# Relative attention layers: five PSUM slots for transposed scores and jobs, one pair of banks for the row-maximum scores

## The chip, the cores and the metric

The kernel runs on one core of a Trainium2 chip. The metric is the device time of one execution in microseconds (us); "the span" is the time from the first to the last instruction of the one execution that was profiled. PE is TensorE, DVE is VectorE, ACT is ScalarE, POOL is GpSimd, SP is the engine that issues most DMAs.

## The reference, cut to what matters

Four attention layers stand one behind the other on 8 images of 32 x 32 tokens with 192 channels, 12 heads of 16. Each adds its result to the stream. Layers 0 and 2 are the relative layers; the change is in them alone:

```
x = x + L0(groupnorm(x)); x = x + L1(...); x = x + L2(groupnorm(x)); x = x + L3(...)
# L0 and L2, per image and head, 1024 queries x 1024 keys, d = 16
attn = (q * d**-0.5) @ k.T + rel_h[query, key row] + rel_w[query, key column]
rel_h = q . Rh[row difference];  rel_w = q . Rw[column difference]
out = softmax(attn) @ v @ w_proj + b_proj
```

## The kernel before, in words

A relative layer is `attend_rel`. Its work is cut into 24 units (`UNITS`): 3 groups of 4 heads times 8 images. The 4 heads of a unit are two pairs (`pr`), and the two heads of a pair (`sd`) lie in the lower and the upper 64 rows of the array. The head's rows hold q and k in split parts and, beside them, the rows of the position tables, so that a score with both tables comes out of two matmuls.

Scores are computed twice. **Straight** scores (`straight`, L1518 and L1524; queries on the partitions) go to the PSUM tensor `S` and serve only for the row maximum: DVE takes it of a pair at once, 128 x 1024 (`row_max`, L1676), and signals `s_done`. **Transposed** scores (`transposed`, L1499 and L1503; keys on the partitions, the negated maximum already added through rows of `QW`) go to slots of the PSUM tensor `T`; ACT takes the exponential out of them into `PROB` (L1777), and `values` (L1537) multiplies it by V into `O`. The straight scores run 12 steps (`AHEAD`) before the transposed ones that need their maximum.

PSUM has eight banks of 512 f32 columns: before, `S` has two pairs, `T` three slots (`RING`), `O` one.

The order of PE is written out by hand in `body`: 16 steps a unit; in each step, first half: transposed, straight, values of the step before; second half: transposed, straight; then the step's jobs from the table `JOBS`. Jobs use slots of `T` too: `qk0`, `qk1`, `v` (projections for unit u + 2, L1545 and L1553), `rel0` to `rel3` (position tables, L1564 and L1568, evicted by ACT at L1794 and DVE at L1704), `nm..` (transposed maxima, L1577, added to `QW` by DVE at L1707), and the tail of the unit before: `sel` (L1585, reciprocal at L1717), `inv` (L1590, product into `OSB` at L1720), `wo` (output projection, L1597, copied to `Y` by ACT at L1798). Steps 0, 8 and 15 have no job. The list `ORDER` gives every transposed score and job a number, and `slot` is that number modulo `RING`; `free` makes PE wait until what was in the slot is evicted, by ACT (`t_act`) or DVE (`t_dve`). `pad` takes a number and issues nothing.

Before the units stand `START`, the projections and tables of units 0 and 1, and in `nm00` 16 straights in a row, then 8 more (`prologue`). All engines run the units two at a time in a loop, with the first two and last two written out.

SP's `section` brings the data of the next units in a fixed order: the q lines for the tables (`QC`, after `qk1`; `rel0` waits for them), images and weights, storing the parts, query rows, storing the position tables that POOL has permuted (L1373), table rows, keys, and again query and table rows. POOL works in order too: V, the wide inverse (L1379), the split of q and k, the permutations, the output's accumulating DMAs.

The waits of PE that the change touches are these:

```
need(pe, s_done, 32 * w_ + 2 * m + pr - 1)     # straight: the maximum of the straight before the last
pe.wait_ge(out_of[k], value)                   # free: the slot's last user
```

Of the kernel before, what the change touches and what calls it, by code (L numbers as in the profile page):

```python
# [12 lines left out]
P = 128  # L13
# [1077 lines left out]
def attend_rel(nc, sems, name, xn, stream, w, ident):  # L1091

    UNITS = GROUPS * IMAGES
    STEPS = 2 * CHUNKS
    RING, PRING = 3, 2
    VARIANTS = 4
    EIGHT = SIDE // VARIANTS
    SPLITS = 4
# [1 line left out]

    JOBS = {1: ("sel1", "qk0"), 2: ("qk1",), 3: ("inv1", "v"), 4: ("nm10", "nm11"), 5: ("rel0",), 6: ("wo10",),
            7: ("rel1", "wo11"), 9: ("rel2",), 10: ("sel0",), 11: ("rel3", "inv0"), 12: ("nm00", "nm01"), 13: ("wo00",),
            14: ("wo01", "pad")}
    ORDER = [n for s in range(STEPS) for n in
             [("st", s, pr, sd) for pr in range(2) for sd in range(2)] + list(JOBS.get(s, ()))]
    AT = {n: i for i, n in enumerate(ORDER)}
# [3 lines left out]
    MADE = {"qk0", "qk1", "v", "rel0", "rel1", "rel2", "rel3"}  # L1110
    SKIP = {0: TAIL1, UNITS - 2: MADE, UNITS - 1: MADE | {"nm00", "nm01"}, UNITS: set(ORDER) - TAIL1}
    START = [(n, v) for v in range(2) for n in ("qk0", "qk1", "v", "rel0", "rel1", "rel2", "rel3")] + [("nm00", 0)]
    START += [("nm01", 0), ("pad", 0), ("pad", 0)]
    assert len(START) % RING == 0
    assert len(ORDER) % RING == 0

# [30 lines left out]
    with ExitStack() as ctx:  # L1147
# [7 lines left out]

            return ap.bitcast(F32)

        S = ctx.enter_context(nc.psum_tensor(f"{name}_S", [P, 2, 2, BANK], F32))
        T = ctx.enter_context(nc.psum_tensor(f"{name}_T", [P, RING, BANK], F32))
        O = ctx.enter_context(nc.psum_tensor(f"{name}_O", [P, BANK], F32))  # L1160
        QV = sb("QV", [P, 2, 2, VARIANTS, TOKENS], F32R)
# [303 lines left out]
        def _(pe):  # L1465
            def free(u, *names, maxima=None):

                latest = {}
                for n in names:
                    v, i = u, AT[n] - RING  # L1470
                    while i < 0 or ORDER[i] not in used(v):
                        if i < 0:
                            v, i = u - 1, i + len(ORDER)
                            if isinstance(u, int) and u == 0:
                                break
                        else:
                            i -= RING
                    started = isinstance(u, int) and u == 0 and v is not u
                    for k in ("act", "dve") if started else (kind(ORDER[i]),):
                        at = -1 if started else i - (0 if v is u else len(ORDER))  # L1480
                        if k not in latest or at > latest[k][0]:
                            latest[k] = at, base(0, k) if started else upto(v, ORDER[i], k)
                waits = {k: value for k, (_, value) in latest.items()}
                if maxima is not None and "dve" not in waits:
                    waits["dve"] = upto(u, "nm11", "dve") if maxima else (
                        begun("nm01", 0, "dve") if isinstance(u, int) and u == 0 else upto(u - 1, "nm01", "dve"))
                elif maxima is not None:
                    assert latest["dve"][0] >= (AT["nm11"] if maxima else AT["nm01"] - len(ORDER))
                for k, value in waits.items():
                    pe.wait_ge(out_of[k], value)  # L1490

            def transposed(u, par, s, pr):
                qh, kc = divmod(s, CHUNKS)
# [12 lines left out]
            def straight(w_, par, m, pr):  # L1506

                c, kh = divmod(m, 2)
                need(pe, s_done, 32 * w_ + 2 * m + pr - 1)
                if pr == 0 and m == 0:  # L1510
                    pe.wait_ge(k_moved, KEY_ROWS * (w_ + 1))
                if pr == 0 and m % 8 == 0:
                    pe.wait_ge(rows_moved[m // 8], ROWS * (w_ + 1))
                alone(pe)
                queries = slice(P * c, P * c + P)
                for sd in range(2):
                    lines = slice(64 * sd, 64 * sd + 64)
                    nc.tensor.matmul(S[:, pr, sd], QW[lines, par, pr, queries], KW[lines, kh * BANK:(kh + 1) * BANK],  # L1518
                                     start=True, stop=False)
                for kq in range(2):  # L1520
                    here, keys = slice(256 * kq, 256 * kq + 256), slice(BANK * kh + 256 * kq, BANK * kh + 256 * kq + 256)
                    for sd in range(2):
                        lines = slice(64 * sd, 64 * sd + 64)
                        last = nc.tensor.matmul(S[:, pr, sd, here], QV[lines, par, pr, 2 * kh + kq, queries],  # L1524
                                                KV[lines, par, pr, keys], start=False, stop=kq == 1)
                        if kq:
                            last.then_inc(s_ready, 1)
# [52 lines left out]
            def tail(u, half, which, to, ready):  # L1580
                if which == "sel":
                    pe.wait_ge(o_out, 2 * u + half + 1)
                    alone(pe)
                    for c in range(4):
                        last = nc.tensor.transpose(T[:, to, P * c:P * c + P], OSB[:, P * c:P * c + P], ident_sb[:])  # L1585
                elif which == "inv":
                    pe.wait_ge(widened, 2 * u + half + 1)
                    alone(pe)
                    for c in range(4):
                        last = nc.tensor.transpose(T[:, to, P * c:P * c + P], inverse_wide[:, P * c:P * c + P], ident_sb[:])  # L1590
                else:
                    m = int(which[2])
                    if m == 0:
                        pe.wait_ge(t_dve, ready)
                        pe.wait_ge(wo_loaded, 16 * (u + 1))
                    alone(pe)
                    last = nc.tensor.matmul(T[0:HALF, to], wo_sb[:, m * HALF:(m + 1) * HALF], OSB[:], start=True, stop=True)  # L1597
                last.then_inc(t_ready, 1)

            def job(u, par, n):  # L1600
                if n not in used(u):
                    return
                free(u, n)
                to = slot(n)
                if n[:2] == "qk":
                    project(u + 2, int(n[2]), to)
                elif n == "v":
                    project_v(to)
                elif n[:3] == "rel":
                    relative(u + 2, int(n[3]), to)  # L1610
                elif n[:3] == "nm1":
                    turn_max(u, 1, int(n[3]), to)
                elif n[:3] == "nm0":
                    turn_max(u + 1, 0, int(n[3]), to)
                else:
                    half = int(n[-2] if n[:2] == "wo" else n[-1])
                    which = "wo" + n[-1] if n[:2] == "wo" else n[:3]
                    tail(u - half, half, which, to, upto(u, f"inv{half}", "dve") if which == "wo0" else None)

            def prologue():  # L1620
                pe.wait_ge(consts_loaded, CONSTS)
# [49 lines left out]
        def _(eng):  # L1671
            def row_max(w_, m, pr):
                c, kh = divmod(m, 2)
                qh, c = divmod(c, 4)
                eng.wait_ge(s_ready, 64 * w_ + 4 * m + 2 * pr + 2)
                nc.vector.tensor_reduce(nmp[:, qh, c, 2 * pr:2 * pr + 2, kh], S[:, pr], AX.X, ALU.max).then_inc(s_done, 1)  # L1676

            def combine(w_, qh):

# [1039 lines left out]
```

## Time and profile before

| | |
|---|---|
| median of 3 runs | 9231.04 us (9228.94 to 9237.27) |
| the profiled execution | 9223.04 us, span 9221.4 us |
| PE busy | 7542.9 us, 82% of the span |
| DVE busy | 5284.4 us, 57% |
| ACT busy | 4527.8 us, 49% |
| POOL busy | 2587.1 us, 28% |
| row maxima (L1676) | 1536, 1224 ns each, 1878.3 us |
| exponentials (L1777) | 3072, 595 ns each, 1667.3 us |

Busy time is what an engine's own instructions took. An idle time in front of an instruction is put down to what ended it (`<-`); "issue" is an idle time that the profile gives no releaser for. Matmuls are pipelined: the shown time of one is longer than the spacing of two, and where several rows of one kind follow each other they are merged (`x2`). The granted clock is the share of full speed that TensorE had: 1.00 is 2.4 GHz and 0.50 is 1.2 GHz.

### The profile page before, as it was taken

The numbers are of one execution on the slowest core, as the hardware profiler recorded it, in microseconds if no ns is written. First come the engines' busy times: TensorE is split into PE (matmuls) and PEld (weight loads), VectorE is DVE, ScalarE is ACT, GpSimd is POOL, SyncE is SP. The second block draws the span as 40 slices with busy tenths as digits, with TensorE's granted clock in tenths as the row PEclk, the third lists the DMA queues.
The fourth block names the chain that finished last, engine by engine and source line by source line (L and its number), as shares of the span: only waits on it lengthen the run. The fifth ranks groups of instructions, "written<-read, shape, count | busy, mean of one in ns | idle before, by whom it ended". The sixth has DMA issues, their size and how long they took to land. (4 is left out here: it accounts for less than half of the span.)

```text
span 9221.4 us, 201937 instructions
## 1 busy us (share of the span) xinstructions
PE 7542.9 (82%) x68440; PEld 4564.9 (50%) x68440; DVE 5284.4 (57%) x7803; ACT 4527.8 (49%) x8209; POOL 2587.1 (28%) x2843
## 2 busy tenths in 40 slices
PE   2988889889388878846889888888576699999999
PEld 2555555555155555524555555554232355555555
DVE  3555555555255555544555555554677477777776
ACT  1444444444265655632444444445233377777776
POOL 2343434333021121114433333342455300000000
PEclk7899999999698999977999998999677799999999
DMA  6666666665433333346665665664221344444443
GB/s 160 130 119 135 122 130 118 130 123 105 112 70 68 75 70 71 74 118 126 126 128 120 122 126 118 123 117 74 92 72 62 88 123 112 126 111 123 115 122 82
DMA packets 536710, 999.89 MB, mean 108 GB/s; under 512 B 102129, under 2 KB 303026, under 8 KB 500210
## 3 DMA queue, kind: packets, MB, share of 16 engines
q1 hardware_dynamic: 479346, 900.57, 43.6%
q0 software_dynamic: 56576, 88.90, 6.2%
q8 instruction: 485, 7.95, 0.4%
q14 instruction: 303, 2.48, 0.1%
HBM read 646.02 MB, written 335.81 MB: 106 GB/s over the span
## 5 line engine op out<-in xcount | busy, mean ns | idle before, releaser
L1676 DVE TENSOR_REDUCE a_nmp<-a_S 128x2 f32<-128x1024 f32 x1536 | 1878.3, 1224 | 1433.6 <-PE a_S L1524 1430.5
L1777 ACT ACTIVATE a_PROB<-a_T 128x512 f32<-128x512 f32 x3072 | 1667.3, 595 | 1977.5 <-PE a_T L1503 1964.2
L1373 POOL CAST a_RF<-a_RL 32x512 fp32r<-32x512 f32 x1536 | 1295.2, 843 | 1011.8 <-DVE a_RL L1704 919.9
L2498 DVE CUSTOM_DVE_ANT_0 a_X<-a_S,a_mask 128x1024 f32<-128x1024 f32 x768 | 909.3, 1221 | 608.7 <-PE a_S L2413 593.4
L2531 ACT ACTIVATE a_PROB<-a_T 128x512 f32<-128x512 f32 x1536 | 918.2, 598 | 439.1 <-PE a_T L2426 429.3
L1499 PE MATMUL a_T<-a_QW,a_KW 64*128 64x512 f32 x3072 | 801.1, 514 | 402.0 <-issue 149.1
L2426 PE MATMUL a_T<-a_ident,a_X 128*128 128x128 f32 x6144 | 994.6, 285 | 32.2 <-DVE a_OSB L2511 16.5
L1499 PEld LDWEIGHTS a_T<-a_QW,a_KW 64*128 64x128 f32 x3072 | 311.3, 191 | 1427.1 <-issue 1424.2
L1537 PE MATMUL a_O<-a_PROB,a_V 128*32 128x512 f32 x6144 | 887.8, 652 | 2.9 <-ACT a_PROB L1777 2.5
L962 DVE CUSTOM_DVE_ANT_0 a_PROB<-a_S,a_mask 128x512 f32<-128x512 f32 x768 | 522.9, 688 | 598.5 <-PE a_PT L799 505.8
L2426 PEld LDWEIGHTS a_T<-a_ident,a_X 128*128 128x128 f32 x6144 | 660.0, 141 | 327.1 <-issue 305.5
L1524 PEld LDWEIGHTS a_S<-a_KV,a_QV 64*128 64x128 f32 x6144 | 652.1, 199 | 116.8
L1518 PE MATMUL a_S<-a_KW,a_QW 64*128 64x512 f32 x3072 | 662.8, 418 | 27.3 <-DVE a_nmp L1676 27.3
L1503 PE MATMUL a_T<-a_QV,a_KV 64*128 64x512 f32 x3072 | 648.0, 409 | 35.1 <-issue 35.1
L1524 PE MATMUL a_S<-a_KV,a_QV 64*128 64x256 f32 x6144 | 660.9, 290 | 0.0
L2438 PE MATMUL a_O<-a_PROB,a_V 128*32 128x128 f32 x12288 | 655.0, 284 | 2.0 <-ACT a_PROB L2531 0.5
L2369 POOL DMA_DIRECT2D out<-a_Y x96 | 92.0, 959 | 1845.6 <-ACT a_PROB L2531 1832.5
L1043 ACT ACTIVATE a_PROB<-a_PROB,a_nmax 128x512 f32<-128x512 f32 x768 | 550.4, 719 | 76.1 <-DVE a_nmax L962 76.1
L1564 PE MATMUL a_T<-a_QC,a_tab_d 16*32 16x64 f32 x6144 | 414.3, 300 | 181.9 <-issue 106.0
L799 PE MATMUL a_PT<-a_ident,a_PROB 128*128 128x128 f32 x3072 | 491.8, 285 | 50.4 <-ACT a_PROB L1043 31.0
L1564 PEld LDWEIGHTS a_T<-a_QC,a_tab_d 16*32 16x32 f32 x6144 | 362.8, 127 | 207.8 <-issue 186.5
L2550 ACT ACTIVATE a_X<-a_X,a_rmax 128x1024 f32<-128x1024 f32 x384 | 438.6, 1142 | 38.0 <-DVE a_rmax L2498 38.0
(160 smaller groups left out, 10640.8 us busy)
## 6 DMA issues: line engine op xcount, KB each, us to landing
a_QV<-a_part_rows SPq DMA_DIRECT2D x384, 256.0 KB, 7.1
a_rel_rows<-a_RF SPq DMA_DIRECT2D x96, 1024.0 KB, 9.2
a_K<-part_rows SPq DMA_DIRECT2D x576, 128.0 KB, 3.3
a_X<-xn_scratch SPq DMA_DIRECT2D x72, 768.0 KB, 6.4
stream<-a_Y POOLq DMA_DIRECT2D x288, 192.0 KB, 5.7
a_part_rows<-a_part SPq DMA_DIRECT2D x48, 1024.0 KB, 11.8
a_QV<-a_part_rows SPq DMA_DIRECT2D x384, 128.0 KB, 7.7
a_QV<-a_rel_rows SPq DMA_DIRECT2D x384, 128.0 KB, 7.4
```

Source lines behind the costliest of these rows:

```text
L1373: nc.gpsimd.tensor_copy(dst, src).then_inc(permuted, 1)
L1499: nc.tensor.matmul(T[:, slot(("st", s, pr, sd))], KW[lines, keys], QW[lines, par, pr, cols], start=True, stop=False)
L1518: nc.tensor.matmul(S[:, pr, sd], QW[lines, par, pr, queries], KW[lines, kh * BANK:(kh + 1) * BANK], start=True, stop=False)
L1524: last = nc.tensor.matmul(S[:, pr, sd, here], QV[lines, par, pr, 2 * kh + kq, queries], KV[lines, par, pr, keys], start=False, stop=kq == 1)
L1537: last = nc.tensor.matmul(O[Q * g:Q * g + Q], V[:, par, kc, g], PROB[:, s % PRING, g], start=kc == 0, stop=kc == CHUNKS - 1)
L1564: last = nc.tensor.matmul(T[at + 32:at + 64, to, 64 * a:64 * a + 64], tab_d[:, x], QC[:, :, half * BANK + x:(half + 1) * BANK:SIDE], start ...
L1676: nc.vector.tensor_reduce(nmp[:, qh, c, 2 * pr:2 * pr + 2, kh], S[:, pr], AX.X, ALU.max).then_inc(s_done, 1)
L1777: nc.scalar.activation(PROB[:, s % PRING, 2 * pr + sd], T[:, slot(("st", s, pr, sd))], ACT.Exp).then_inc(t_act, 1)
L2426: last = nc.tensor.transpose(T[:, slot(("t", s)), P * g:P * g + P], X[:, par, c, g, P * kc:P * kc + P], ident_sb[:])
L2438: last = nc.tensor.matmul(O[Q * g:Q * g + Q, par, P * c:P * c + P], V[:, par, kc, g], PROB[:, s % PRING, g], start=kc == 0, stop=kc == CHU ...
L2498: nc.vector.tensor_tensor_reduce(out=X[:, v % 2, c, g], in0=S[:, sd].rearrange("p a b -> p (a b)"), in1=mask[:, n % 2, g, c], scale=1.0, s ...
L2531: nc.scalar.activation(PROB[:, s % PRING].rearrange("p g x -> p (g x)"), T[:, slot(("t", s))], ACT.Exp, scale=-1.0).then_inc(t_act, 1)
```

## The change

`RING` goes from 3 to 5 and `S` from two pairs of banks to one; `O` keeps its bank, so all eight are used as before. `straight` now waits for the maximum of the straight just before it. `ORDER` and `START` get pads so that their lengths divide by five. The wait of the first output projection for the product in `OSB` is left out where the slot's own wait already covers it. No arithmetic and no DMA changes.

```diff
-    RING, PRING = 3, 2
+    RING, PRING = 5, 2
-            14: ("wo01", "pad")}
+            14: ("wo01", "pad", "pad")}
-    START += [("nm01", 0), ("pad", 0), ("pad", 0)]
+    START += [("nm01", 0)] + [("pad", 0)] * 4
-        S = ctx.enter_context(nc.psum_tensor(f"{name}_S", [P, 2, 2, BANK], F32))
+        S = ctx.enter_context(nc.psum_tensor(f"{name}_S", [P, 2, BANK], F32))
         T = ctx.enter_context(nc.psum_tensor(f"{name}_T", [P, RING, BANK], F32))
...
             def straight(w_, par, m, pr):
-                need(pe, s_done, 32 * w_ + 2 * m + pr - 1)
+                need(pe, s_done, 32 * w_ + 2 * m + pr)
...
-                    nc.tensor.matmul(S[:, pr, sd], QW[lines, par, pr, queries], KW[lines, kh * BANK:(kh + 1) * BANK],
+                    nc.tensor.matmul(S[:, sd], QW[lines, par, pr, queries], KW[lines, kh * BANK:(kh + 1) * BANK],
...
-                        last = nc.tensor.matmul(S[:, pr, sd, here], QV[lines, par, pr, 2 * kh + kq, queries],
+                        last = nc.tensor.matmul(S[:, sd, here], QV[lines, par, pr, 2 * kh + kq, queries],
...
                     if m == 0:
-                        pe.wait_ge(t_dve, ready)
+                        if ready is not None:
+                            pe.wait_ge(t_dve, ready)
...
-                nc.vector.tensor_reduce(nmp[:, qh, c, 2 * pr:2 * pr + 2, kh], S[:, pr], AX.X, ALU.max).then_inc(s_done, 1)
+                nc.vector.tensor_reduce(nmp[:, qh, c, 2 * pr:2 * pr + 2, kh], S[:], AX.X, ALU.max).then_inc(s_done, 1)
```

## Rows read from the trace of the kernel before

**Rows 1.** Windows: the first relative layer; busy us, then granted clock, DMA share, GB/s.
```profile
200.00:2330.00 2130.00, 1880.34 (x16588) 1160.96 (x16588) 1184.00 (x1302) 934.72 (x1715) 824.28 (x1001) 0.93 0.63 122
```

**Rows 2.** Waits of PE, units 0 to 21, first layer: us, times, longest.
```profile
PE a_T L1499 <- DVE a_QW L1707: 40.6, 40, 1.0
PE a_T L1564 <- DMA a_QC<-a_whole: 31.7, 8, 5.4
PE a_T L1499 <- DVE a_RL L1704: 28.4, 37, 1.0
PE a_T L1499 <- ACT a_PROB L1777: 21.7, 77, 0.8
PE a_T L1499 <- ACT a_Y L1798: 18.4, 22, 0.8
```

**Rows 3.** Waits of PE in the second relative layer, 4275 to 6310 us.
```profile
PE a_T L1564 <- DMA a_QC<-a_whole: 44.2, 11, 5.5
```

**Rows 4.** Waits of PE in unit 15 of the first layer, 1598.7 to 1687.9 us.
```profile
PE a_T L1499 <- DVE a_QW L1707: 2.0, 2, 1.0
PE a_T L1499 <- DVE a_RL L1704: 1.6, 2, 1.0
PE a_T L1499 <- ACT a_PROB L1777: 1.1, 4, 0.3
PE a_T L1499 <- ACT a_Y L1798: 0.8, 1, 0.8
```

**Rows 5.** Timeline of PE in the same unit: start, us, what, idle before.
```profile
1601.53 0.39 PE L1518 MATMUL a_S<-a_KW,a_QW 64*128 64x512 f32 x2
...
1602.47 0.50 PE L1499 MATMUL a_T<-a_QW,a_KW 64*128 64x512 f32 x2 [0.30 <-ACT a_PROB L1777]
...
1603.01 0.43 PE L1518 MATMUL a_S<-a_KW,a_QW 64*128 64x512 f32 x2
...
1605.17 0.40 PE L1518 MATMUL a_S<-a_KW,a_QW 64*128 64x512 f32 x2
...
1625.95 0.50 PE L1499 MATMUL a_T<-a_QW,a_KW 64*128 64x512 f32 x2 [1.01 <-DVE a_QW L1707]
```

**Rows 6.** Timeline of DVE there; the first QW addition alone, then both merged.
```profile
1602.24 1.23 DVE L1676 TENSOR_REDUCE a_nmp<-a_S 128x2 f32<-128x1024 f32 x1 [0.93 <-PE a_S L1524]
...
1625.13 0.68 DVE L1707 TENSOR_TENSOR a_QW<-a_T,a_QW 128x512 fp32r<-128x512 f32 x1
1625.13 1.28 DVE L1707 TENSOR_TENSOR a_QW<-a_T,a_QW 128x512 fp32r<-128x512 f32 x2
```

**Rows 7.** Timelines of POOL, SP (DMA issues) and PE, units 14 and 15.
```profile
1575.05 14.42 POOL L1373 CAST a_RF<-a_RL 32x512 fp32r<-32x512 f32 x16
...
1603.24 2.50 SPq L1289 DMA_DIRECT2D a_QV<-a_rel_rows  x4
...
1618.37 2.48 SPq L1260 DMA_DIRECT2D a_QC<-a_whole  x4
...
1634.07 0.28 PE L1564 MATMUL a_T<-a_QC,a_tab_d 16*32 16x64 f32 x1 [4.79 <-DMA a_QC<-a_whole]
```

**Rows 8.** Timeline of PE in the prologue, two of the straights that wait.
```profile
214.27 0.80 PE L1518 MATMUL a_S<-a_KW,a_QW 64*128 64x512 f32 x2 [0.28 <-DVE a_nmp L1676]
...
216.90 0.80 PE L1518 MATMUL a_S<-a_KW,a_QW 64*128 64x512 f32 x2 [0.28 <-DVE a_nmp L1676]
```

**Rows 9.** Windows: the prologue's straights, and the second layer's last unit.
```profile
211.00:243.00 32.00, 26.40 (x136) 20.25 (x136) 27.21 (x29) 0.00 (x0) 12.19 (x15) 0.50 0.53 109
6384.00:6448.00 64.00, 48.57 (x322) 19.78 (x320) 12.54 (x18) 37.12 (x69) 5.12 (x8) 0.98 0.10 14
```

**Rows 10.** Waits of PE in the second layer's last two units, 6310.5 to 6448 us.
```profile
PE a_T L1499 <- ACT a_PROB L1777: 10.3, 16, 1.3
```

**Rows 11.** Timeline of PE after rel0 of unit 15: one half-step at low clock.
```profile
1636.26 0.80 PE L1499 MATMUL a_T<-a_QW,a_KW 64*128 64x512 f32 x2
...
1640.12 0.50 PE L1499 MATMUL a_T<-a_QW,a_KW 64*128 64x512 f32 x2
```

More of the change, by code:

```diff
@@ L1490, in free @@
                     pe.wait_ge(out_of[k], value)
+                return {k: at for k, (at, _) in latest.items()}
             def transposed(u, par, s, pr):
@@ L1602, in job @@
                     return
-                free(u, n)
+                freed = free(u, n)
                 to = slot(n)
@@ L1617, in job @@
                     which = "wo" + n[-1] if n[:2] == "wo" else n[:3]
-                    tail(u - half, half, which, to, upto(u, f"inv{half}", "dve") if which == "wo0" else None)
+                    tail(u - half, half, which, to, upto(u, f"inv{half}", "dve")
+                         if which == "wo0" and freed.get("dve", -len(ORDER)) < AT[f"inv{half}"] else None)
             def prologue():
```

## The prediction

> **What bounds the kernel now.** I read the windows by stage first. Everything the change touches lies in the two relative layers, the first of them some 2130 us of the 9221 us span, the other much the same; in the first, PE is busy 1880 of 2130 us at a granted clock of 0.93 [rows 1]. So PE's own instruction order is the clock of the stage, and the question is only which of its idle time goes and what comes. The waits of PE give the idle time by cause [rows 2, 3]. For units 0 to 21 of the first layer the short waits in front of the transposed scores (L1499) are for a PSUM slot: 40 for a QW addition, 37 for an RL subtraction, 77 for an exponential, 22 for a Y copy; 109 us in 176 waits. The same view shows 8 waits for the QC rows at L1564 (31.7 us), and in the second layer 11 (44.2 us): places where a DMA chain, not PE, sets the time. Then I went through one unit instruction by instruction. One unit is 16 steps of two half-steps; a half-step is transposed, straight, and in the first half also values.
>
> **Part 1, three slots to five: slot waits go.** Unit 15 of the first layer (1598.7 to 1687.9 us) has nine of them: 2.0 + 1.6 + 1.1 + 0.8 = 5.5 us of idle [rows 4]. After such a wait the pipelined overlap with the matmul before is lost too: the straight scores at 1601.53 would let the next transposed start 0.57 later (the spacing without a wait), at 2.10, and it starts at 2.47, so 0.30 of shown idle costs 0.37 [rows 5]. With 0.07 for each wait a full unit pays 6.1 us. With five slots the pair of a half-step needs what was issued four and five places back, which has always been evicted for a microsecond or more in these rows, so I take all of it as gone. By place: step 7 to 8 0.62, 8 to 9 0.37, 10 to 11 0.28, 11 to 12 1.10, 12 to 13 1.08, 14 to 15 0.91, 15 to 0 0.37, 0 to 1 0.37, 4 to 5 1.07. The two pads and the conditional wait before wo00 cost nothing: a pad issues no instruction, and the dropped wait is implied by the slot's.
>
> **Part 2, one pair of score banks: a new wait.** Each straight now waits for the row maximum of the straight just before it. On PE nothing passes a waiting instruction: behind it stand the values, the next transposed scores, and so ScalarE's exponentials. The loop is: straight start 1601.53 to maximum start 1602.24, 0.71; the maximum 1.23 by itself; its end to the next matmul 0.15 (the first QW addition at 1625.13 takes 0.68 and the transposed that waits for it starts at 1625.95) [rows 5, 6]. Sum 2.09 us.
> - First to second half: straight at 1603.01 to straight at 1605.17 is 2.16 (values lie between) [rows 5]. 2.09 fits, by 0.07.
> - Second half to the next step's first, no job between: 0.57 + 0.57 = 1.14. New stall 0.95. Steps 0, 8 and 15 have no job. After a stall the straight's own first matmuls are spaced wider (the fill, as above), 0.08, so 1.03 each.
> - With a job of about 1 us or more (qk, v, rel, nm, wo) it fits. Only sel0 in step 10 is short: bounds 0.28 (its wait now) and 1.03, I take 0.53, as its four transposes cover about half.
> - DVE's queue: where a job's eviction stands in front of a maximum, that maximum is late. The two QW additions together end at 1625.13 + 1.28 = 1626.41 [rows 6], while the maximum of the straight that would now run a microsecond earlier could start at about 1626.16: 0.25 late, and the second half stalls 0.2 + 0.08. That is twice a unit (steps 5, 13); the RL subtraction does the same after rel0, rel2 and rel3, 0.15 to 0.24 + 0.08.
>
> Per unit, steps 5 to 10: gone 0.99, new 0.23 + 1.03 + 0.23 = 1.49, so **+0.5 us**; in the even units the step 7 wait is often not there now, so +0.65 as a mean. Steps 10 to 5: gone 5.18, new 0.53 + 0.32 + 0.29 + 1.03 + 1.03 + 0.29 = 3.49, so **-1.7 us**; in units after the loop's jump (PE idle up to 9 us between steps 15 and 0, which covers that stall) -2.4.
>
> **What hides it.** POOL's permutation of the last tables starts at 1575.05, just after sel0's reciprocal, and takes 14.4; the table rows are issued at 1603.24, after their store, SP then issues keys and query rows and reaches the QC rows at 1618.37; rel0 waits 4.79 for them until 1634.07 [rows 7]. From step 10 to step 5 that unit is set by POOL and DMA, not PE. A PE saving there only lengthens this wait. The wait exists 8 + 11 = 19 times [rows 2, 3]; I count 20 with one near zero. So of 44 steady units the -1.7 or -2.4 counts in 24: 18 after a jump, 18 x 2.4 = 43, and about 4 others, 7: **-50 us**. The +0.65 counts in all 44: **+29 us**.
>
> **Prologue.** Here 16 and then 8 straights stand back to back. Now every second one waits 0.28 for the maximum two back, and pairs are 216.90 - 214.27 = 2.63 apart [rows 8]. That period is already the full loop (matmul, maximum, matmul) at the granted clock of 0.50, the 1.2 GHz level [rows 9]; with one pair of banks it passes one straight, not two. 16 straights: last maximum 15 x 2.63 instead of 7 x 2.63 plus 1.14 behind the first: +20. The 8 after it: 7 x 2.63 less what they take now (about 9 to 10.5): +9. I see nothing that covers it: DVE and PE alternate and unit 0 begins behind it. If the clock were at the upper level the loop would be 2.09 and the sum +17. Two layers: **+57 us** (bounds +34, +60).
>
> **The last two units** of a layer have no rel, qk or v, so fewer covers: unit 22 stalls at six bare steps. But unit 23 has no straights from step 4 on, and there the slot waits are large, up to 1.3 us; the view lists some 22 us in all for the pair, of which the largest row is shown [rows 10]. New waits I put at 13 with the values' wait for the exponential. **-10 us** a layer, -20 (bounds -6, -30).
>
> **Clock.** Low-clock stretches follow rel jobs and are longest where the 1 us slot waits come next (step 12). These waits go; I take **-8 us** (bounds -36, +20). A low step costs 1640.12 - 1636.26 = 3.86 us from transposed to transposed in the first half, where the rows at full clock give 2.13 [rows 11].
>
> **Sum.** +57 + 29 - 50 - 20 - 8 = +8 us on the profiled execution's 9223.04 (span 9221.4). The runs' median is 9231.04, 8 above it, so the same sum gives 9239; I write 9238.
>
> The Trainium skill (Perfetto Trace Analysis, Matmuls) says that independent matmul groups should rotate through different PSUM banks, so that the eviction of one overlaps the matmuls of the next. It speaks against this change: applied strictly, each straight would pay its whole maximum. The trace agrees for the prologue and for steps without a job only; with values or a job between, PE has other banks' work.
>
> **Rivals.**
> A. *The 0.07 us margin is not there* (slower). In 16 places a unit a straight follows its maximum by almost exactly the loop. The 0.15 is read at transposed scores and may be longer for a straight, whose weights can't be fetched ahead while it waits. For: it is a margin of 3% on modelled matmul ends. Against: the waits in the prologue show the same 0.15. It decides above 0.22. At 0.10 over, 16 + 5 places cost 2.1 us a unit, half of it hidden in 20 units: 44 x 2.1 - 20 x 1.1 = +70, 9308. Chance 0.22.
> B. *The clock falls in steps 15, 0, 1 and 8* (slower). Three low steps add at least 1.7 us each and lose half their stall: +3.6 a unit, some hidden, +110: 9348. Against: in the last unit PE idles 1.3 us in steps of 3.9, and the granted clock is 0.98 [rows 9, 10]. Chance 0.07. The Trainium skill (TensorE: Matmul & The Clock Gate, "A second HAM failure mode: psum-queue depth-cycling") tells of a kernel whose small idles between matmul groups made the clock swing; by that this rival is the case, by the row it is not.
> C. *Less is hidden* (faster). The QC wait has 1.1 to 6 us and may shrink if PE's earlier steps 15 and 2 let SP issue keys and QC rows sooner; then up to 20 x 1.7 = 34 us more is kept, and if the low steps at 12 vanish another 28: 9238 - 62 = 9176, half of it 9207. For: SP's keys wait for step 15. Against: they are issued behind the table rows of 1603.24, while step 15's straight is that of 1601.53 or before [rows 5, 7], so the stores set them. Chance 0.26.
> D. *The change doesn't do what it says*: slots are not what L1499 waits for, but the QW rows themselves. Then only the prologue and the stalls count, of which I take 3 us a unit as not under those waits: 9231 + 57 + 44 x 3 = 9420. Against: the waits end at the first of two QW additions, in a step whose rows need neither. Chance 0.03.
>
> **Numbers.** Forecast 0.42, own range 9215 to 9265; A 0.22, B 0.07, C 0.26, D 0.03. "Same" means within 0.2% (18 us, about what a measurement here tells from no change), 9213 to 9249: forecast 0.30, A 0.04, C 0.04: 0.38. Faster: C 0.22, forecast 0.03: 0.25. Slower: 0.37. The range reaches into A and C: 9190 to 9300.
>
> **What would show it.** Short waits at L1499 for QW, RL, PROB and Y nearly gone; new waits of L1518 for nmp, about 3 of 0.9 us a unit; QC waits longer by 1 to 2 us each; first unit of each layer begins 28 to 30 us later in its layer. Wrong if straights in second halves wait too (A), or the stage's granted clock moves by over 0.02 (B, C).

## The result, and the profile after

The changed kernel takes **9312.03 us** (median; 9300.15 to 9328.08) against 9229.99 us of the kernel before on the same chip: a ratio of **1.0093, 95% interval 1.0073 to 1.0113**. It is 0.93% slower, 12 us outside the range and 74 us above the forecast. The profiled execution took 9315.44 us, its span 9313.8 us, at a mean granted clock of 0.894 (before 0.900).

Lines of the page after, answering to the table of before: busy us, mean ns of one, idle time in front and what ended most of it.

```profile
PE 7577.8 (81%) x68440; PEld 4471.8 (48%) x68440; DVE 5266.3 (57%) x7803; ACT 4518.2 (49%) x8209; POOL 2591.1 (28%) x2843
...
L1679 DVE TENSOR_REDUCE a_nmp<-a_S 128x2 f32<-128x1024 f32 x1536 | 1879.2, 1223 | 1456.4 <-PE a_S L1525 1453.9
L1780 ACT ACTIVATE a_PROB<-a_T 128x512 f32<-128x512 f32 x3072 | 1669.5, 597 | 1955.1 <-PE a_T L1504 1935.9
...
L1565 PE MATMUL a_T<-a_QC,a_tab_d 16*32 16x64 f32 x6144 | 416.0, 300 | 276.5 <-DMA a_QC<-a_whole 151.2
```

DVE and ACT do what they did. The last line is the one to mark: the idle time in front of the tables' matmuls, put down to the transfer of the QC rows. Before, that was 75.9 us in the two layers [rows 2, 3].

Windows of the first relative layer after, answering to [rows 1]. The stretch is 37 us longer, and its granted clock is 0.90 where it was 0.93:

```profile
200.00:2367.00 2167.00, 1892.52 (x16404) 1113.36 (x16402) 1158.64 (x1284) 915.69 (x1687) 824.28 (x998) 0.90 0.63 119
```

Waits of PE after in units 0 to 21 of the first layer (273.8 to 2304.1 us): us in total, times, longest. They answer to [rows 2].

```profile
PE a_T L1500 <- issue: 88.5, 9, 11.3
PE a_T L1565 <- DMA a_QC<-a_whole: 70.6, 11, 7.8
PE a_S L1519 <- DVE a_nmp L1679: 58.6, 81, 1.0
PE a_T L1565 <- issue: 6.5, 1, 6.5
```

And in the second relative layer (4374.8 to 6410.5 us), answering to [rows 3]:

```profile
PE a_T L1500 <- issue: 79.8, 9, 10.6
PE a_T L1565 <- DMA a_QC<-a_whole: 76.7, 11, 9.0
PE a_S L1519 <- DVE a_nmp L1679: 59.3, 86, 1.0
```

One row of this layer before (units 0 to 21, 4272.6 to 6309.2 us) stands in none of the groups above and has nothing that answers to it after. It is a second idle time of 3 to 5 us in the step behind each of the nine jumps:

```profile
PE a_T L1503 <- issue: 35.1, 9, 5.0
```

Every slot wait of [rows 2] is gone. In their place stands about half as much time for the row maximum; the QC rows take over twice as long in the first layer (77 us for 32), and there are 9 long idles in front of L1500, which are the loop's jumps. One odd unit of the first layer (1655 to 1743 us), answering to [rows 4], shows the same in small:

```profile
PE a_T L1565 <- DMA a_QC<-a_whole: 5.1, 1, 5.1
PE a_S L1519 <- DVE a_nmp L1679: 3.0, 4, 1.0
```

**Where the 92 us between the two spans are.** I set the start of each unit in one trace against the other. The table's numbers are sums and differences of such times (a unit starts at its first L1500, and the last two end with the last product in `OSB`).

| | before | after | difference | predicted |
|---|---|---|---|---|
| first unit of layer 0 begins at | 243.9 | 273.8 | +30.0 | +28.5 |
| first straight of layer 2 to its first unit | 44.7 | 74.4 | +29.7 | +28.5 |
| units 0 to 21, layer 0 | 1993.7 | 2030.3 | +36.6 | |
| units 0 to 21, layer 2 | 2036.5 | 2035.7 | -0.9 | |
| both | 4030.2 | 4066.0 | **+35.7** | **-29** |
| last two units, both layers | | | -16.5 | -20 |
| everything else | | | +13.5 | 0 |

The last line is the rest of the sum and lies in code that the change leaves alone, for the most part in the window layer between the two; no run here explains it. The prologue and the last units came nearly as predicted. The forecast had 8 us and the spans differ by 92; of the 84 us between, 65 are in the 44 steady units and 14 in that last line.

### The profile page after: what moved, and what is told of

It is laid out like the page before. It is cut to its first block and busy times, and to the rows that moved or that the text cites. A ratio compares the mean times of both kernels' runs of the same rounds, so it can differ in the third digit from the quotient of the medians.

```text
span 9313.8 us, 201407 instructions
## 1 busy us (share of the span) xinstructions
PE 7577.8 (81%) x68440; PEld 4471.8 (48%) x68440; DVE 5266.3 (57%) x7803; ACT 4518.2 (49%) x8209; POOL 2591.1 (28%) x2843
## 5 line engine op out<-in xcount | busy, mean ns | idle before, releaser
L1500 PE MATMUL a_T<-a_QW,a_KW 64*128 64x512 f32 x3072 | 794.4, 511 | 171.6 <-issue 169.2
L1519 PE MATMUL a_S<-a_KW,a_QW 64*128 64x512 f32 x3072 | 710.5, 450 | 221.7 <-DVE a_nmp L1679 218.3
L1500 PEld LDWEIGHTS a_T<-a_QW,a_KW 64*128 64x128 f32 x3072 | 304.2, 192 | 1154.4 <-issue 1151.0
L1525 PEld LDWEIGHTS a_S<-a_KV,a_QV 64*128 64x128 f32 x6144 | 677.3, 200 | 73.1
L1519 PEld LDWEIGHTS a_S<-a_KW,a_QW 64*128 64x128 f32 x3072 | 343.4, 199 | 513.8 <-issue 465.3
```

The lines of the kernel that those rows point to most:

```text
L1500: nc.tensor.matmul(T[:, slot(("st", s, pr, sd))], KW[lines, keys], QW[lines, par, pr, cols], start=True, stop=False)
L1519: nc.tensor.matmul(S[:, sd], QW[lines, par, pr, queries], KW[lines, kh * BANK:(kh + 1) * BANK], start=True, stop=False)
L1525: last = nc.tensor.matmul(S[:, sd, here], QV[lines, par, pr, 2 * kh + kq, queries], KV[lines, par, pr, keys], start=False, stop=kq == 1)
```

## The experiments

Times are medians, "before" is the kernel before on the same chip. The changed kernel stands at 1.0093 in this measure.

| | time | before | ratio, 95% interval |
|---|---|---|---|
| e1 one pair of score banks, still three slots | 9374.33 | 9219.12 | 1.0163 (1.0132 to 1.0193) |
| e2 after, prologue with two pairs of banks | 9260.07 | 9219.12 | 1.0035 (1.002 to 1.0049) |
| e3 before, short permutations | 9095.56 | 9219.12 | 0.9856 (0.9825 to 0.9886) |
| e4 after, short permutations | 9037.08 | 9219.12 | 0.9796 (0.9766 to 0.9825) |
| e5 before, PE's loop written out | 9133.56 | 9229.7 | 0.9908 (0.9886 to 0.993) |
| e12 as e2, PE's loop written out | 9162.2 | 9227.02 | 0.9937 (0.992 to 0.9953) |
| e6 before, SP's order changed | 9079.34 | 9229.7 | 0.9847 (0.9829 to 0.9865) |
| e7 e2 with SP's order changed | 9014.1 | 9229.7 | 0.9764 (0.9736 to 0.9792) |
| e8 e7, PE's loop written out | 8916.85 | 9229.7 | 0.966 (0.9641 to 0.968) |
| e9 e7, all compute loops written out | 8814.87 | 9217.95 | 0.9565 (0.9529 to 0.96) |
| e10 e6, all compute loops written out | 8852.74 | 9217.95 | 0.9604 (0.9584 to 0.9625) |
| e11 e9, jobs moved to the bare steps | 8807.66 | 9217.95 | 0.9556 (0.9529 to 0.9583) |

### e1 and e2: the two halves, and the prologue

e1 is the changed kernel with the slots taken back:

```diff
-    RING, PRING = 5, 2
+    RING, PRING = 3, 2
...
-            14: ("wo01", "pad", "pad")}
+            14: ("wo01", "pad")}
...
-    START += [("nm01", 0)] + [("pad", 0)] * 4
+    START += [("nm01", 0), ("pad", 0), ("pad", 0)]
```

> The changed kernel with the slots put back to three and the score banks left at one pair: the new wait alone. Theory 1 (from sel0 in step 10 on, the permutation on POOL, the store of the tables and the DMAs behind it set when rel0 of the next unit or PE's first instruction after the loop's jump can run, so PE's slot waits between step 10 and step 5 were never paid for): only the slot wait in step 7 to 8 comes back, about 0.7 us in 44 units (31 us), and some 16 us in the last two units: 9312 + 47 = about 9360. Rival (PE's order is the clock; the five slots did save some 5 us a unit and the loss is elsewhere): 4.7 us x 44 come back, about 9520.

9374.33 us, 14 above the theory and far from the rival. One pair alone costs 1.63%, and five slots give back 0.70 of those points. Waits of PE in units 0 to 21 of its first layer:

```profile
...
PE a_T L1500 <- DVE a_QW L1710: 39.9, 40, 1.0
PE a_T L1500 <- DVE a_RL L1707: 27.3, 35, 1.0
PE a_S L1519 <- DVE a_nmp L1679: 24.9, 62, 0.7
PE a_T L1500 <- ACT a_Y L1801: 18.4, 22, 0.8
```

The slot waits are those of [rows 2], and the straights wait for less than half as long as with five slots: what three slots cost covers part of what one pair costs. The two halves are not additive.

e2 gives the prologue its second pair of banks back, out of the slots that stand empty there:

```diff
-                need(pe, s_done, 32 * w_ + 2 * m + pr)
+                need(pe, s_done, 2 * m + pr - 1 if early else 32 * w_ + 2 * m + pr)
...
+                bank = T[:, 1:3] if early and pr == 0 else S[:]
```

> The changed kernel, but in the prologue the straights of the first pair go to two banks of the transposed scores' slots that are idle there, so that the 16 and 8 straights alternate between two pairs again. Theory 1: the prologue's 30 us a layer come back whole, 9312 - 58 = 9254. Rival (the later start is absorbed, as the DMAs of units 0 and 1 gain the same time): less than half of it comes back, above 9283.

9260.07 us: 52 less than the changed kernel's 9312 (6 above the theory), and its first unit begins at 243.5, where it began before the change. Two straights of the prologue after, and the maximum in front of the first:

```profile
214.90 0.80 PE L1519 MATMUL a_S<-a_KW,a_QW 64*128 64x512 f32 x2 [1.41 <-DVE a_nmp L1679]
...
217.54 0.80 PE L1519 MATMUL a_S<-a_KW,a_QW 64*128 64x512 f32 x2 [1.41 <-DVE a_nmp L1679]
```

```profile
213.53 1.23 DVE L1679 TENSOR_REDUCE a_nmp<-a_S 128x2 f32<-128x1024 f32 x1 [1.41 <-PE a_S L1525]
```

The period of 2.64 is that of [rows 8], but it now passes one straight instead of a pair. 213.53 + 1.23 = 214.76, and the next matmul starts at 214.90: 0.14 later. Prologue +57: shown, by the start of the first unit and by e2's time.

### e3 and e4: the same change without the long chain

[rows 7] gave the chain POOL, store, SP, QC rows. To see what the slots are worth without it, POOL copies only 8 elements a piece for two of the four tables from unit 2 on, in the kernel before (e3) and in the changed one (e4). So part of the position tables is left out in both.

```diff
+                        if r >= 2 and not (isinstance(v, int) and v < 2):
+                            src, dst = RL[i][lines, r % 2, 0:8], RF[lines, i, 0, 8 * r:8 * r + 8]
-                        if quad % 2 == 0:
+                        elif quad % 2 == 0:
...
```

> The kernel before, but from unit 2 on the 16 permuting copies of rel2 and rel3 copy 8 elements a row instead of 512 (that part of the tables is left out): POOL's part of the chain is about 12 us shorter, its stores and DMAs stay. Theory 1: the waits of rel0 for its rows go (76 us) and PE's idle after the loop's jump, 4 to 9 us eighteen times, shrinks too, as it ends with the tables' store: 9090 to 9140. Rival (the jump's idle is the fetch by itself, PE bounds the rest): only the 76 us go, 9155, and the jump's idle stays.

> The changed kernel with the same part left out. Theory 1: with the chain out of the way the five slots pay: against the kernel before with the same part left out the prologue costs 60, the last two units save 16, and 44 units save about 1.2 us each less some low clock: a difference of 0 to +20 us instead of +82. Rival (the new stalls cost more than the slots save, whatever POOL does): the difference stays +70 or more.

9095.56 and 9037.08: the changed kernel is now 58 us **faster**, although it still carries its prologue. Both the theory (0 to +20) and the rival (+70) miss, the theory on the side of the slots. Units 0 to 21 took 1944.5 + 1980.8 us in e3 and 1888.2 + 1895.4 in e4, so 142 us less. Waits of PE from 230 to 2100 us, e3 and then e4:

```profile
...
PE a_T L1501 <- DVE a_QW L1709: 38.6, 38, 1.0
PE a_T L1501 <- DVE a_RL L1706: 24.1, 32, 1.0
PE a_T L1501 <- ACT a_PROB L1779: 20.0, 70, 0.8
PE a_T L1501 <- ACT a_Y L1800: 17.6, 21, 0.8
```

```profile
PE a_S L1521 <- DVE a_nmp L1681: 76.8, 93, 1.4
PE a_T L1502 <- issue: 56.0, 9, 7.4
...
PE a_T L1567 <- DMA a_QC<-a_whole: 2.0, 2, 1.9
```

(The 76.8 hold the prologue's end too.) The QC wait is gone in e3 and all but gone in e4. In the 44 units PE idles 139 us less in e4 than in e3. Of these, 33 are at the loop's jumps; the other 106 are the exchange, for which the forecast's prices come to some 59. So my price for it was too low, not too high, and what is wrong is how much of it PE may keep while the chain is there. (e4 also has fewer half-steps at 1.2 GHz in these units, 70 for 103.)

### e5 and e12: without the jump

Of the 44 units I counted 24 as PE's own, 18 of them because they follow the loop's jump and show no QC wait. e5 and e12 take the jump out of PE alone, by writing its loop out, in the kernel before and in e2:

```diff
+            if eng is nc.tensor:
+                for u in range(2, UNITS - 2):
+                    body(u, u % 2)
+            else:
                 with eng.Fori(1, UNITS // 2 - 1) as p:
```

> The kernel before with PE's loop over units written out, so that PE never jumps; the other engines keep their loops. Theory 1 (the idle after the jump is a fetch that lands behind the store of the tables, and without it rel0 of the even units meets the same chain as that of the odd ones, 61.7 us from sel0): even units shorten from 66 to 70 us (sel0 to rel0) to 61.7, about 45 us in the first layer and 80 in the second, and the waits for the QC rows appear in even units too: 9219 - 125 = 9095. Rival (the idle after the jump was PE's own and comes back whole): 9219 - 172 = 9047 with no new QC waits.

> The changed kernel with the prologue banks as in e2 and TensorE's loop of the relative layers written out, SP's order as it was. It stands to e5 (the kernel before with TensorE's loop written out, 9133.6 us) as the changed kernel stands to the kernel before, but with no jump of TensorE that could take up a gain. Theory (the wait for the QC rows alone is enough to absorb the slots' gain; the jump is only a second taker): the units as long as in e5, the QC rows waited for by 40 to 90 us more, the whole 9110 to 9160 us. Rival (it was the jump's idle time that took it, the QC chain has slack of its own): the slots' 110 us a layer less 60 of straight waits come through, 40 to 90 us below e5, 9045 to 9095 us, with QC waits as in e5.

e5: 9133.56 us, 39 above its theory. e12: 9162.2 us, 2 above the theory's range and 67 above the rival's. Waits of PE in units 0 to 21 of the first layer, e5 and then e12 (here the view gives "issue" for the wait of the tables' first matmul, L1568 and L1572, for the QC rows, and for most slot waits at L1503 of e5):

```profile
PE a_T L1503 <- issue: 74.2, 86, 1.5
PE a_T L1503 <- ACT a_PROB L1781: 67.6, 88, 6.5
PE a_T L1568 <- issue: 42.6, 9, 6.4
```

```profile
PE a_T L1572 <- issue: 88.5, 17, 9.0
PE a_S L1526 <- DVE a_nmp L1687: 58.2, 81, 1.0
PE a_T L1504 <- ACT a_PROB L1789: 45.2, 9, 5.7
```

In both layers together the QC wait goes from 75 us in 17 units to 178 us in 32 (the theory had 40 to 90 us more), and the units get no shorter (3945.0 in e5, 3976.6 in e12). From sel0 to the next unit's rel0 it takes 59 to 65 us in e5 and 60.3 to 63.9 in e12. But two kinds of units have to be told apart:

- **Into the 22 odd units** the QC wait grows from 62.4 to 149.0 us, and these stretches get 21 us longer in sum. The chain takes the whole gain, and no jump is there.
- **Into the 18 even units behind a jump of the other engines** the QC wait is nothing in e5 and 14.9 us in e12. What PE waits for in their first step is an exponential, as ACT still jumps: 97.0 us in e5 and 89.4 in e12 (the rows of 67.6 and 45.2 are the first layer's; the first of them holds small slot waits too). These stretches get 36 us shorter, 2.0 a unit, where I had forecast 2.4.

So the theory holds for the odd units alone. Behind the jumps most of the gain is kept.

### e6 and e7: the chain cut by SP's order

SP issues the query rows and table rows of a unit's second half in front of the QC rows and the image. e6 moves them behind what the next unit's `rel0` needs:

```diff
+                if not (isinstance(n, int) and n < 2):
+                    query_rows(n - 2, par, 1)
+                    table_rows(n - 2, par, 1)
...
-                query_rows(v, 1 - par, 1)
-                table_rows(v, 1 - par, 1)
...
```

> The kernel before, but SP issues the query and table rows of the second half (needed only eleven steps later) after the next unit's q lines and images instead of before them, so that the QC rows of rel0 don't queue behind them. Theory 1 (the QC rows are late because of what stands before them): the 76 us of waits at rel0 go: 9140. Rival (the DMA queues are full anyway and the rows come as late): above 9200.

> The changed kernel with the prologue's banks and the same order on SP. Theory 1: with the chain to rel0 cut, the five slots pay in the odd units as they did with POOL's part left out, and the low clock after the long waits goes: below the kernel before with the same order by 30 to 60 us, about 9090. Rival (the slots only pay where POOL's copies are gone): equal to or above the kernel before with the same order.

e6: 9079.34 us, 61 below its theory, with no QC wait left. So the order of SP's queue was worth 150 us to the kernel before, three times what I gave the slots. e7 (the same with e2's changes) comes out at 9014.1: 65 below e6, where its theory had 30 to 60 less (and about 9090 in all). From sel0 to rel0 of an odd unit e6 takes mostly 56.8 and e7 54.9 us. Into an even unit, past the jump, both take 64 to 73 us. PE's idle time right behind the jumps, 3 us and more at once, is 61.8 us in e6's first relative layer and 103.1 in its second (35.3 of these a second idle time, as in the kernel before); in e7 it is 87.9 and 83.3. In the first layer it grows, and these stretches stay as long as they were (594 and 596 us for nine); in the second it shrinks, and they get 30 us shorter.

### e8, e9 and e10: the jumps out too

e8 is e7 with the edit of e5. e9 writes out the loops of DVE and ACT as well, and e10 does that to e6:

```diff
-            with eng.Fori(1, UNITS // 2 - 1) as p:
-                body(2 * p, 0)
-                body(2 * p + 1, 1)
+            for u in range(2, UNITS - 2):
+                body(u, u % 2)
```

> As the last, and PE's loop written out. Theory 1: with both limits gone PE's own order sets the time, and the idle after the jump comes back nearly whole: 9090 - 150 = about 8940. Rival: something else in the chain (the tables' store) holds the even units and less than 80 us come.

> The changed kernel with the prologue's banks, SP's new order, and the unit loops of TensorE, VectorE and ScalarE all written out. Theory 1: what still holds the even units is ScalarE's own jump (24 waits of PE for an exponential, 91 us); it goes, 8917 - 80 = about 8840. Rival (another part of the chain holds them at the same place): above 8890.

> The kernel before (three slots, two pairs) with SP's new order and all three loops written out, so that the two layouts of PSUM are compared where neither the chain nor a jump can hide anything. Theory 1: the slot waits now cost what they show; against the five slots with the repaired prologue it is slower by 1.2 us x 44 = 53 for the units, 16 for the last two, and some 40 for low-clock stretches, as with POOL's part left out: about 8945. Rival (the five slots never pay): at or below the other.

8916.85 and 8814.87 us, both some 25 below their theories. In e8 PE waits instead for ACT's jump (90.8 us in 24 waits of up to 5.9 us for the exponential, in both layers together); e9 has none of that. e10 is the miss: 8852.74, 92 below what I expected. e9 is faster by 38 us, but not in the steady units: 1842.3 + 1844.3 us there, 1845.6 + 1835.7 in e10. Windows of 200 to 2100 us, e9 and then e10:

```profile
200.00:2100.00 1900.00, 1821.69 (x16140) 1072.81 (x16142) 1128.93 (x1254) 895.92 (x1652) 805.32 (x974) 0.95 0.67 135
```

```profile
200.00:2100.00 1900.00, 1771.87 (x16112) 1102.54 (x16110) 1135.91 (x1253) 898.57 (x1648) 804.17 (x975) 0.97 0.67 135
```

Nearly the same number of matmuls keeps PE busy 50 us longer in e9, at 0.95 instead of 0.97. Counted half-step by half-step (0.8 us for the first pair of transposed matmuls instead of 0.5) e9 has 43 + 38 at the 1.2 GHz level and e10 21 + 12. At some 1.7 us each [rows 11] the 48 more are an estimated 82 us, against 98 us less idle time in e9's units: with nothing else left, the slots' gain is paid back in clock. e10 has 234.5 us of slot waits in its units and e9 132.0 us of waits for maxima, so the kernel with more small idles has the higher clock. The Trainium skill (TensorE: Matmul & The Clock Gate, "A second HAM failure mode: psum-queue depth-cycling") puts a swinging clock down to small idles between matmul groups; by these two traces their number or sum doesn't decide it. What does stays open.

### e11: the bare steps filled

The stalls stand in steps 0, 8 and 15, which have no job. e11 spreads the jobs:

```diff
-    JOBS = {1: ("sel1", "qk0"), 2: ("qk1",), 3: ("inv1", "v"), 4: ("nm10", "nm11"), 5: ("rel0",), 6: ("wo10",),
-            7: ("rel1", "wo11"), 9: ("rel2",), 10: ("sel0",), 11: ("rel3", "inv0"), 12: ("nm00", "nm01"), 13: ("wo00",),
+    JOBS = {0: ("qk0",), 1: ("sel1", "qk1"), 2: ("v",), 3: ("inv1",), 4: ("nm10", "nm11"), 5: ("rel0",), 6: ("wo10",),
+            7: ("rel1",), 8: ("wo11",), 9: ("rel2",), 10: ("sel0",), 11: ("rel3", "inv0"), 12: ("nm00", "nm01"),
+            13: ("wo00",), 14: ("wo01", "pad", "pad")}
```

> As the first of these three, and the jobs moved so that steps 0 and 8 have one: qk0 to step 0, qk1 to 1, v to 2, wo11 to 8. Theory 1 (a bare step costs about 1.0 us, as its straight waits for the maximum before it): two of three stalls of 1.03 go, step 3 with inv1 alone gains one of 0.5: 44 x 1.5 = 66 less, about 8775. Rival (the stalls only trade places with ScalarE's or the DMAs' time): within 20 us of the first.

8807.66 us, 7 less than e9 and within its interval: by the medians the rival. Waits of PE from 230 to 2100 us, e9 and then e11:

```profile
PE a_S L1524 <- DVE a_nmp L1685: 70.2, 94, 1.0
```

```profile
PE a_S L1524 <- DVE a_nmp L1685: 35.6, 74, 1.0
```

Half of the stalls go, and the medians hardly move. In the two profiled executions the 44 units take 3686.6 us in e9 and 3652.7 in e11, with 139.4 and 77.7 us of idle time. But the execution profiled of e9 was 18 us above its median and that of e11 9 us below, so these 34 us say little more than the medians do. Where the rest of the 62 us of idle time went is open. e9 and e11 are the fastest here, 4.4% below the kernel before.

## Why the prediction was wrong

**The step that failed** is "so of 44 steady units the -1.7 or -2.4 counts in 24: -50 us", and with it the sentence "A PE saving there only lengthens this wait", which put a longer wait at no cost. The stretches of the 44 units, in sum over both layers, show what came instead:

| | before | after | difference | predicted |
|---|---|---|---|---|
| sel0 to rel0, into the 18 even units behind a jump | 1234.0 | 1204.0 | -30 | -43 |
| the same, into the 4 odd units without a QC wait before (one had 0.3 us) | 242.8 | 246.0 | +3 | -7 |
| the same, into the 18 odd units with one | 1109.8 | 1121.8 | +12 | 0 |
| rel0 to sel0, all 44 | 1206.6 | 1256.8 | +50 | +29 |
| the rest (start, into unit 2, end) | 237.0 | 237.5 | +0.5 | 0 |
| clock, a term of its own in the forecast | | | in the rows above | -8 |

All but rel0 to sel0 came to -14 where the prediction had -50.

- *The odd units.* It took "no QC wait here" for "PE has room here". The four odd units without one took 60.7 us each from sel0 to rel0, no less than the others (61.7 on average), and after the change all 22 wait, 4.1 to 9.0 us. Why the other 18 got 0.7 us longer each is open.
- *The units behind a jump* kept 30 of their 43 us. In e2, whose units are the same code, they took 1192.6 us, which is 41 less than before. So this part of the term was nearly right.
- *From rel0 to sel0* PE's idle time grew by 8 us only (36.6 to 44.8). The half-steps at 1.2 GHz went from 48 to 78 there, an estimated 51 us at 1.7 each. This stretch begins behind the QC wait that "only lengthens".

The chain can be measured on both sides of the change. Timelines of POOL, SP and PE after, units 14 and 15, answering to [rows 7]:

```profile
1632.81 14.45 POOL L1373 CAST a_RF<-a_RL 32x512 fp32r<-32x512 f32 x16
...
1660.51 1.72 SPq L1289 DMA_DIRECT2D a_QV<-a_rel_rows  x4
...
1675.95 2.48 SPq L1260 DMA_DIRECT2D a_QC<-a_whole  x4
...
1691.76 0.28 PE L1565 MATMUL a_T<-a_QC,a_tab_d 16*32 16x64 f32 x1 [5.10 <-DMA a_QC<-a_whole]
```

From POOL's start to rel0 it is 1691.76 - 1632.81 = 58.95 us; before, 1634.07 - 1575.05 = 59.02 [rows 7]. PE's own work in between got shorter and this stretch did not. The chain starts from PE's sel0 and ends in the next unit's rel0, so into an odd unit it closes as a loop, with a nearly fixed length of some 62 us from sel0 to rel0, and PE keeps only what changes from rel0 to sel0. There the change costs time.

In even units a jump stands in between. PE's timeline after, around one of them:

```profile
1742.48 0.50 PE L1500 MATMUL a_T<-a_QW,a_KW 64*128 64x512 f32 x2
...
1743.05 0.43 PE L1519 MATMUL a_S<-a_KW,a_QW 64*128 64x512 f32 x2
...
1754.05 0.80 PE L1500 MATMUL a_T<-a_QW,a_KW 64*128 64x512 f32 x2 [10.33 <-issue]
...
1757.92 0.79 PE L1500 MATMUL a_T<-a_QW,a_KW 64*128 64x512 f32 x2
...
1761.44 0.50 PE L1519 MATMUL a_S<-a_KW,a_QW 64*128 64x512 f32 x2 [0.96 <-DVE a_nmp L1679]
```

The 10.33 us of this jump were 9.3 before, in front of the unit that follows the one of [rows 4]. In sum over both layers the idle time behind the 18 jumps is 165.4 us before, with the second idle times of the second layer, and 168.3 after. It is no taker of the gain as a whole, but it moved, and I had taken it as given: in the first layer it grew from 71.2 to 88.5 us, and the stretches into even units stayed as long as they were (-2 us); in the second it shrank from 94.2 to 79.8, and they got 28 us shorter.

The records of single DMA packets in the two traces tell what ends it. In front of all 36 restarts a packet of queue q8, kind "instruction", 16 KB, had ended 1.7 to 2.7 us earlier, and in front of all nine ends of a second idle time one had ended 1.3 to 1.8 us earlier. In front of the 44 odd units, where PE doesn't jump, there is none at that distance. So PE very likely waits there for its next instructions; no experiment here changes that alone, and what makes the packet come later after the change is open.

Point by point:

- **Part 1, slot waits go, -6.1 a unit: right.** 230.2 us of them before, none after.
- **Part 2, the loop of 2.09 us: right at the bare steps.** The stalls behind steps 0, 8 and 15 are 0.92 to 0.95 on average, as in the last row above. **Too dear elsewhere:** behind sel0 it is 0.17 for a forecast of 0.53, and of the forecast 0.2 to 0.3 behind QW and RL jobs five waits of 0.24 show in 44 units. So the exchange is worth more than I said, about -110 us of idle time in 44 units (230 less 118) instead of some -59; e4 shows it.
- **"The +0.65 counts in all 44", +29: +50.** The place was right, as this is the stretch outside the chain; the cause was not. The bare step and sel0 account for less than the forecast, and the rest is low clock. After QC waits of 7 us and more rel0 to sel0 takes 30.2 us on average (12 units, 3.0 low half-steps each), after shorter ones 28.4 (12 units, 1.75), after none 27.7 (20 units, 1.05); before, the average was 27.4. Without those waits the same change makes this stretch 6 us longer in both layers (e3 to e4) or 17 (e6 to e7). That the longer wait brings the low clock fits all this but isn't the only cause: e9 has 50 low half-steps there and e10 14, and neither has a QC wait.
- **Prologue +57: +59.7.** Last two units -20: -16.5, no exception.
- **Clock -8: wrong sign.** Half-steps at 1.2 GHz in the units went from 111 to 127; at some 1.7 us each [rows 11] that is an estimated +28. Step 12 has 13 fewer, as predicted; steps 6, 8 and 10 have 30 more. The prediction's own sign, a stage's granted clock that moves by over 0.02, came in the stretch of [rows 1] (0.93 to 0.90), where the longer prologue at 1.2 GHz has a share; the units alone went from 0.93 to 0.91 and stayed at 0.92.
- **Rival A** named 9308, and the run gave 9312, but its mechanism isn't there. PE's timeline in unit 15 after, answering to [rows 5]:

```profile
1656.79 0.50 PE L1519 MATMUL a_S<-a_KW,a_QW 64*128 64x512 f32 x2 [0.95 <-DVE a_nmp L1679]
...
1679.39 0.39 PE L1519 MATMUL a_S<-a_KW,a_QW 64*128 64x512 f32 x2
...
1681.51 0.45 PE L1519 MATMUL a_S<-a_KW,a_QW 64*128 64x512 f32 x2
...
1683.71 0.40 PE L1519 MATMUL a_S<-a_KW,a_QW 64*128 64x512 f32 x2
```

  1679.39 to 1681.51 are 2.12 us with the values between, and no wait is shown. Of the 167 waits for a maximum in the 44 units seven are of a straight in a second half, so the margin of 0.07 holds. A number that agrees is no evidence for a cause.
- **Rival B** (the clock falls in steps 15, 0, 1 and 8) has a part in it: step 8 has 18 low half-steps for 11. Steps 15, 0 and 1 have no more than before, and most of the new ones follow rel0 and rel2. **Rival C** asked the right question, how much the QC wait hides, with the sign wrong: the wait grew. **D** is excluded by the waits.

On the rule of the Trainium skill (Perfetto Trace Analysis, Matmuls) to rotate independent groups through PSUM banks: it spoke against the change and, for the prologue's 60 us and the bare steps' 2.9 us a unit, the trace agrees. Steps with values or a job between two straights pay nothing. But what made the kernel slower was not that alone: with the chain shortened (e3, e4) the same exchange of banks wins.

## What to carry to other kernels

Before a saving on the busiest engine is counted, measure the leg, which is the time between the two places where a chain of other engines and DMAs leaves it and comes back, in every iteration. If that leg is the same length with and without a visible wait, the engine is not the bound there, even where it never waits; the saving is worth only what falls outside the leg. Don't price the longer wait at nothing either: look at the clock behind it. And add up all idle times behind a loop's jump before you compare two kernels: by one row of the waits view alone the jumps look 38 us dearer here (168.3 for 130.3), and with the second row they are 3 us dearer.

Break such a chain first and weigh buffers after that: here the order of one DMA queue was worth 150 us and written-out loops another 227, while the same change of banks cost 82 us in front of the chain, gained 65 with the chain cut and the prologue mended (e7 against e6), and 38 us, none of it in the units, once the loops were written out (e9 against e10).

## What the hardware showed that was not expected

- The idle time at a loop's jump on PE is 4 to 15 us over these runs (14.8 once in e1), not constant, and in the waits view it has no cause. A 16 KB packet of the instruction queue q8 ends 1.7 to 2.7 us before PE goes on, in all 36 jumps of the two kernels. With the loops written out on PE, DVE and ACT the idle time is gone: e9 is 199 us below e7.
- After the long idle time PE comes back at 1.2 GHz (0.80 at 1754.05, after 10.33 idle); after the short one it stays at 2.4 GHz (0.50 at 1656.79, after 0.95). So a wait that grows can cost more than its own length.
- Clock and small idle times: a granted clock of 0.97 (200 to 2100 us) with 234 us of idle times of at most 1.5 us in 44 units (e10), and 0.95 with 132 us (e9).
